# Attention groups with the shift added by TensorE and copied by ScalarE, and another order of the chunks at the end

## What is computed

```python
def _L1_xattn_ref(decoder_input, encoder_output, W_q, W_k, W_v, W_o, b_o):
    Q = (decoder_input @ W_q).reshape(B, Sd, HEADS, HEAD_DIM)      # 16 heads of 8
    K = (encoder_output @ W_k).reshape(B, Se, HEADS, HEAD_DIM)
    V = (encoder_output @ W_v).reshape(B, Se, HEADS, HEAD_DIM)
    scores = jnp.einsum('bqhd,bkhd->bhqk', Q, K) / jnp.sqrt(jnp.float32(HEAD_DIM))
    attn = jax.nn.softmax(scores, axis=-1)
    out = jnp.einsum('bhqk,bkhd->bqhd', attn, V).reshape(B, Sd, E)
    return out @ W_o + b_o

def _L1_ffn_ref(x, kernel, input_scale, kernel_scale, bias):
    x_q = (x / s_in).astype(jnp.float8_e4m3fn)
    k_q = (kernel / s_k).astype(jnp.float8_e4m3fn)
    y = jnp.dot(x_q, k_q) * (s_in * s_k)
    return y.astype(bfloat16) + bias
...
x = x + _L1_xattn_ref(_layernorm(x), ctx_1024, ...)
x = x + _L1_ffn_ref(_layernorm(x), ...)
```

## Time and profile before

| what | us |
|---|---|
| median of 3 runs | 194.49 |
| lowest and highest | 193.78 and 196.1 |
| the profiled execution | 194.31 |
| its span, first to last instruction | 192.5 |

### The profile page before, as it was taken

How to read it: one execution, slowest core, us unless ns; L and a number is a source line. 1 busy time by engine, 2 the same in 40 slices (tenths; PEclk the granted TensorE clock), 3 DMA queues, 4 the chain that set the end, 5 groups by cost and what they waited for, 6 DMA issues and landing times.

```text
span 192.5 us, 3676 instructions
## 1 busy us (share of the span) xinstructions
PE 173.8 (90%) x1301; PEld 131.7 (68%) x1301; DVE 138.2 (72%) x405; ACT 94.7 (49%) x170; POOL 48.1 (25%) x59
## 2 busy tenths in 40 slices
PE   4599999899999999999999999977999899889771
PEld 4289589678878888888788788553555565545540
DVE  2859757858556755585555697777999999977793
ACT  2357369554431332226322176567566657576252
POOL 3453356370400000028012136170221000002400
PEclk9969999999999999999999999999999999999978
DMA  5994000003084000000023000100230000000003
GB/s 192 370 420 178 2 3 2 0 0 112 3 200 124 5 0 0 0 3 0 0 67 89 11 0 2 58 0 0 73 95 5 0 0 5 0 3 0 0 0 109
DMA packets 5105, 10.26 MB, mean 53 GB/s; under 512 B 1472, under 2 KB 2752, under 8 KB 4800
## 3 DMA queue, kind: packets, MB, share of 16 engines
q1 hardware_dynamic: 3360, 9.44, 15.1%
q10 hardware_dynamic: 1728, 0.60, 1.2%
HBM read 6.37 MB, written 0.52 MB: 36 GB/s over the span
## 4 chain that ended last, share of the span: by engine, by line
PE 64%; issue 10%; DVE 10%; ACT 8%; DMA 4%; POOL 1%; SPq 1%; DVEq 0%; POOLq 0%; ACTq 0%
PE banks L1204 13%; PE bank L1020 6%; PE bank L1022 6%; PE bank L1021 6%; PE bank L1233 4%; DMA ctx<-in_ctx 4%; ACT raw L511 4%; ACT heads_out L519 2%; PE bank L1282 2%; PE banks L1020 2%; PE banks L1021 2%; PE banks L1022 2%; PE bank L1204 2%; PE bank L1273 2%; PE banks L1259 2%
## 5 line engine op out<-in xcount | busy, mean ns | idle before, releaser
L480 ACT ACTIVATE att<-bank 128x512 f32<-128x512 f32 x32 | 19.1, 598 | 46.0 <-PE bank L1022 33.1
L877 DVE TENSOR_REDUCE negm<-bank 128x2 f32<-128x512 f32 x61 | 39.1, 686 | 3.1 <-PE bank L1233 3.1
L511 ACT ACTIVATE raw<-banks 128x1024 f32<-128x1024 f32 x32 | 31.0, 1021 | 13.0 <-PE banks L1259 12.9
L277 POOL TENSOR_TENSOR rstd<-vpe,expo 128x4 f32<-128x4 f32 (+1 forms) x9 | 9.0, 998 | 56.0 <-DVE vpe L643 56.0
L1020 PE MATMUL bank<-xT,w 128*128 128x512 f32 x48 | 20.2, 420 | 0.7 <-DVE xT L774 0.7
L1233 PE MATMUL bank<-kst,w 32*128 32x256 f32 x122 | 20.1, 306 | 0.5 <-DVE negm L877 0.5
L1204 PEld LDWEIGHTS banks<-raw,attT 128*128 128x128 f32 x160 | 19.2, 192 | 1.2 <-issue 0.5
L1204 PE MATMUL banks<-raw,attT 128*128 128x128 f32 x160 | 19.7, 276 | 0.0
L1022 PE MATMUL bank<-xT,w 128*128 128x512 f32 x48 | 18.8, 392 | 0.0
L1021 PE MATMUL bank<-xT,w 128*128 128x512 f32 x48 | 18.8, 391 | 0.0
L845 DVE SCALAR_TENSOR_TENSOR xs<-banks,rw,xs 128x128 f32<-128x128 f32 x52 | 14.6, 344 | 5.7 <-PE banks L1204 5.6
(11 more groups left out here) (204 smaller groups left out, 328.5 us busy)
## 6 DMA issues: line engine op xcount, KB each, us to landing
raw<-in_w SPq DMA_DIRECT2D x1, 2048.0 KB, 10.8
raw<-kx SPq DMA_DIRECT2D x12, 128.0 KB, 2.6
raw<-qx SPq DMA_DIRECT2D x24, 64.0 KB, 2.1
raw<-in_w SPq DMA_DIRECT2D x1, 1024.0 KB, 8.5
xs<-in_x SPq DMA_DIRECT2D x2, 256.0 KB, 3.1
ctxT<-in_ctxT SPq DMA_DIRECT2D x1, 512.0 KB, 5.3
ctx<-in_ctx SPq DMA_DIRECT2D x1, 512.0 KB, 7.4
raw<-in_fixed SPq DMA_DIRECT2D x1, 512.0 KB, 4.0
```

The source lines that it names most:

```text
L480: act.activation(silus[:, k, :], bk[2 * k][:, :], ACT.Silu).then_inc(S["silu_s"], 1)
L511: act.activation(probs[:, m % 2, 2 * r:2 * r + 2, :, :].rearrange("p h k q -> p (h k q)"), pair[r][:, :], ACT.Exp, scale=ATT_SCALE).then_i ...
L877: dve.tensor_reduce(negm[:, m % 2, :, c0:c0 + 1].rearrange("p t c -> p (t c)"), bk[score_bank(m, r)][:, :].rearrange("p (t k) -> p t k", t ...
```

## The change

In a group, TensorE first lays the stacked queries into the bank of the turned maxima (a 256-column matmul with an fp32r identity, when the third maxima of the group are done), then adds the turned maxima to them as two ordinary matmuls. ScalarE copies the sum to `qa`, as the first thing of its group. The second and third scores stand directly behind the turned maxima, ahead of bank 7's work, and VectorE takes the second and third maxima together, ahead of the addition or the normalising. `o_copy(1)` stands ahead of the third normalisation in group 2. At the end the middle chunk goes ahead of the last one in every step, VectorE scales it (`middle_v`) in place of ScalarE, and the four `fill` matmuls between the chunks are gone.

```diff
-ORDER = (0, 2, 1)
+ORDER = (0, 1, 2)
...
+        identr = sb("identr", [P, P], r32)
...
+            act.copy(identr[:, :], ident).then_inc(S["identr_s"], 1)
...
+            def shifted(m):
+                act.wait_ge(S["mT_ps"], m + 1)
+                if m >= 2:
+                    act.wait_ge(S["s2_ps"], 2 * (m - 1))
+                act.copy(qa[:, m % 2, :], bk[turning(m)][:, 0:SEQ]).then_inc(S["qa_s"], 1)
+
             def act_group(m):
                 b, g = m // G, m % G
+                shifted(m)
                 if m == 1:
                     experts_out(UNITS - 2)
...
                 exps(m, 0)
                 exps(m, 1)
+                if m >= 2:
+                    o_copy(m - 1)
                 if m == 2:
                     for t in range(*HALVES[1]):
                         third_scaled(t)
-                if m >= 2:
-                    o_copy(m - 1)
...
             chunk_norm(1)
             turned_out(BATCH - 1)
-            chunk_v(1)
             chunk_overflow(0)
+            chunk_overflow(1)
             chunk_v(2)
             chunk_turned(0)
             chunk_overflow(2)
-            chunk_overflow(1)
             chunk_scaled(0)
+            chunk_turned(1)
             chunk_turned(2)
-            chunk_turned(1)
+            chunk_scaled(1)
             chunk_scaled(2)
-            chunk_scaled(1)
...
-            def shifted(m):
-                dve.wait_ge(S["mT_ps"], m + 1)
-                if m >= 2:
-                    dve.wait_ge(S["s2_ps"], 2 * (m - 1))
-                cols = slice(m // G * SEQ, (m // G + 1) * SEQ)
-                dve.tensor_tensor(qa[:, m % 2, :], bk[turning(m)][:, 0:SEQ], plain(qst[:, m % G, cols]), ALU.add)\
-                    .then_inc(S["qa_s"], 1)
...
                 if more:
                     maxima(m + 1, 0)
-                shifted(m)
                 if m == 2:
                     weigh_last()
                     sum_moments(HALVES[1])
                 if more:
-                    maxima(m + 1, 1)
+                    maxima(m + 1, 1, 2)
                 if g == 0 and b >= 2:
                     add_attention(b - 2, slice(TPB * (b - 2), TPB * (b - 1)))
                 if b > 0 and g in (1, 2):
                     normalise(b - 1, g - 1)
-                if more:
-                    maxima(m + 1, 2)
                 if m == G:
                     queries_lo(1)
                 if more:
...
+            def middle_v():
+                cols = slice(CHUNKS[1][0] * P, CHUNKS[1][1] * P)
+                dve.wait_ge(S["ln4_act"], TPB)
+                dve.tensor_scalar(fv[:, cols], f16[:, cols], rs[:, 0:1], None, ALU.mult).then_inc(S["fv1_s"], 1)
...
             chunk_power(0)
+            middle_v()
+            chunk_power(1)
             add_attention(BATCH - 1, slice(NT - TPB, NT))
             moments(4, CHUNKS[2], lambda t: dve.wait_ge(S["x3_s"], BATCH))
             chunk_rounded(0)
-            chunk_power(1)
+            chunk_rounded(1)
             scaled(4, 2, CHUNKS[2], f16t)
             chunk_overflowed(0)
             chunk_power(2)
             chunk_rounded(2)
-            chunk_rounded(1)
+            chunk_overflowed(1)
             chunk_overflowed(2)
-            chunk_overflowed(1)
...
+            def lay_queries(m):
+                pe.wait_ge(S["s1_max"], 4 * m + 3)
+                if m == 0:
+                    pe.wait_ge(S["identr_s"], 1)
+                    pe.wait_ge(S["hid_s"], HB * UNITS)
+                pe.matmul(bk[turning(m)][:, 0:SEQ], identr[:, :], qst[:, m % G, m // G * SEQ:(m // G + 1) * SEQ],
+                          start=True, stop=False)
+
             def turn_maxima(m):
                 pe.wait_ge(S["s1_max"], 4 * (m + 1))
-                if m == 0:
-                    pe.wait_ge(S["hid_s"], HB * UNITS)
                 for t in range(TPB):
-                    ins = pe.transpose(bk[turning(m)][:, t * P:(t + 1) * P], negm[:, m % 2, t, :], ident)
+                    ins = pe.matmul(bk[turning(m)][:, t * P:(t + 1) * P], negm[:, m % 2, t, :], ident,
+                                    start=False, stop=t == TPB - 1)
...
                 more, final = m + 1 < GROUPS, m == GROUPS - 1
+                lay_queries(m)
                 turn_maxima(m)
                 if more:
                     scores(m + 1, 1)
+                    scores(m + 1, 2)
                 bank7_used(m)
-                if more:
-                    scores(m + 1, 2)
...
             chunk_turn(0)
             chunk_product(0)
-            fill(6, 4)
+            chunk_turn(1)
             chunk_turn(2)
-            chunk_turn(1)
+            chunk_product(1)
             chunk_product(2)
-            chunk_product(1)
```

More of the change, by code:

```diff
@@ L203, in build @@
         names = """
-          ld_x0 ld_x1 ld_ctx ld_const ld_small ld_wc ld_fk ld_bl ld_wl ld_wg ld_w12 ld_w3 ld_att stored setup ident16_s v_zero w12_hi w12_lo k_ps k_out k_hi k_lo fixed staged0 staged1 staged2 staged3 kst_s qst_s
+          ld_x0 ld_x1 ld_ctx ld_const ld_small ld_wc ld_fk ld_bl ld_wl ld_wg ld_w12 ld_w3 ld_att stored setup ident16_s identr_s v_zero w12_hi w12_lo k_ps k_out k_hi k_lo fixed staged0 staged1 staged2 staged3 kst_s qst_s
           wg_hi wg_lo v_ps v_ev bl_added stats_s var_s mean_s rstd_s ln1     ln2
@@ L211, in build @@
           s1_ps s1_max mT_ps qa_s s2_ps p_s v_s pv_ps o_ev oT_ps den_s ao_s aoT_ps aoT_ev wo_ps x3_s
-          rs_s kv_s kovf_s fv_s q_s ovf_s f_s r_s r_pool nmr_s xq_s fT_ps fT_ev f_ps y_s
+          rs_s kv_s kovf_s fv_s fv1_s q_s ovf_s f_s r_s r_pool nmr_s xq_s fT_ps fT_ev f_ps y_s
           yz_s out_s""".split()
@@ L584, in chunk_v @@
                 cols = slice(CHUNKS[c][0] * P, CHUNKS[c][1] * P)
[L585 to L588, removed]
+                act.wait_ge(S["ln4"], TPH + TPB * (c // 2))
                 act.activation(fv[:, cols], f16[:, cols], ACT.Copy, scale=rs[:, 0:1]).then_inc(S["fv_s"], 1)
@@ L974, in shift @@
                     .then_inc(S["nmr_s"], 1)
+            def middle_v():
+                cols = slice(CHUNKS[1][0] * P, CHUNKS[1][1] * P)
+                dve.wait_ge(S["ln4_act"], TPB)
+                dve.tensor_scalar(fv[:, cols], f16[:, cols], rs[:, 0:1], None, ALU.mult).then_inc(S["fv1_s"], 1)
             def chunk_power(c):
                 cols = slice(CHUNKS[c][0] * P, CHUNKS[c][1] * P)
-                power_of_two(fv[:, cols], fe[:, cols], "fv_s", c + 1, 2 * (c + 1))
+                scaled_s, count = ("fv1_s", 1) if c == 1 else ("fv_s", c // 2 + 1)
+                power_of_two(fv[:, cols], fe[:, cols], scaled_s, count, 2 * (c + 1))
             def chunk_rounded(c):
```

## The result

The changed kernel takes 200.0 us (median of 4 runs, 199.66 to 200.94) against 194.1 us: ratio 1.032, 95% interval 1.028 to 1.037. It is slower, where 193.8 us had been forecast. The profiled execution (200.94 us, the longest of the four) has a span of 199.2 us.

The account below looks back on a forecast made before the run. Two near-equal loops, ScalarE's through the third scores and VectorE and TensorE's through the turn, were taken to bound the attention groups. Attention +0.85 and the end -1.4 gave -0.55 us: 193.8 us, range 191.0 to 196.2.

Parts of the forecast that it names:

- two loops of nearly one length: Attention groups: ScalarE's loop through third scores to exponentials; the turn, scores, maxima, `ao`, outputs loop with 0.18 us slack.
- The order: Groups 5 to 15: normalising after third maxima starts outputs 0.24 to 0.3 us later; period 3.82 us against 3.64.
- The kind with g = 3: A batch's group where nothing is normalised: the turn comes 1.14 us behind the outputs' start, period 3.04 us.
- The turned maxima are ordinary matmuls now ... So I count nothing.: TensorE's turn: ordinary fp32 matmuls take 0.12 us against 0.11 for transposes, so no cost; at most 0.05 for weight loads.
- With 0.12 us for that matmul.: Queries' matmul on TensorE, ahead of the turn: 0.12 us taken, between bounds of 0.11 and 0.31.
- Rival 2: TensorE between outputs and second scores pays the added matmul in full: 0.29 us more a group, 197.2 us; chance 0.13.
- Rival 3: At the turn, maxima as ordinary matmuls cost four times a transpose: +7.9 us, 201.7 us; chance 0.02.
- Rival 1: ScalarE's loop stays the limit in the attention groups: 0.14 us a group gained, 191.3 us; chance 0.28.
- The end, -1.4 us: Last chunks: without the fill holding TensorE, VectorE's last addition ends at 188.82 instead of 190.23.
- -0.4 from the order remains: The end: if the removed fill matmuls weren't the holder, the new chunk order alone still saves 0.4 us.
- 0.9 fills it and delays nothing: The end: middle chunk's scaling and power of two, 0.9 us, fit VectorE's 0.97 us wait before L904.
- Groups 0 to 4: Early groups, TensorE the limit: sum's copy delays group 2's last unit by 0.71; about -0.2 us by group 5's turn.

Follow-up runs that it names:

- order_only: Kernel before, with only second and third scores together on TensorE and second and third maxima together on VectorE: ratio 1.001.
- lay_only: Kernel before, with only the queries' matmul added ahead of each turn, its result overwritten by the transposes: ratio 0.999.
- turn_matmul: Kernel before, with only the turned maxima made by ordinary matmuls in place of transposes: ratio 1.006.
- order_turn_matmul: Kernel before, with the new order of second and third scores and maxima plus turned maxima as ordinary matmuls: ratio 1.013.
- early_third: Kernel before, with only TensorE's third scores moved ahead of bank 7's work, VectorE's order kept: 192.4 us, ratio 0.987.
- order_lay: Kernel before, with the new order of second and third scores and maxima plus the queries' matmul, overwritten by the transposes: ratio 1.010.
- end_only: Kernel before, with only the changed end (middle chunk first, its scaling on VectorE, no fill between the chunks): ratio 1.0015.
- after_pool_later: Changed kernel, with GpSimd's addition for chunk 0 waiting until the middle chunk's power of two is made: 199.0 us, ratio 1.029.

## Why the prediction was wrong

*What bounds the kernel before.* Right: two loops of nearly one length. The 1.02 us from the outputs to the next full-array matmul and the 0.18 us of slack are borne out by order_only and lay_only.

*The order.* Right in mechanism, and in size for the groups that it walked through: 3.82 us a group had been worked out with 0.12 for the queries' matmul, so 3.70 without it; order_only has 3.76. `ao` ended 2.68 behind the turn there, where the text had 2.63. The kind with g = 3 was too cheap: 3.04 - 0.12 = 2.92 had been said, and order_only has 3.16. In all the text has 36.34 - 1.2 = 35.1 us for groups 5 to 15 with the order alone, and 36.1 were measured.

*"The turned maxima are ordinary matmuls now ... So I count nothing."* This is the step that failed. The 0.12 us that I took for an ordinary fp32 matmul came from "1.98 us for 16", and I took the 16 rows for 16 matmuls. Line 1204 issues 8, not the 16 that the text on the kernel has: four tiles, two halves of the hidden features. Each is two rows in the trace, so 0.23 us against 0.11 for a transpose. Everything needed stood in view: x16 in the row, two loops in the code. The trace of before even has the very case, the two ordinary fp32 matmuls of `output_layer`, with the 0.71 us that the turn takes in turn_matmul:

```profile
146.81 0.71 PE L1295 MATMUL bank<-wo,aoT 128*128 128x128 f32 x4 [0.19 <-ACT heads_out L519]
```

The same holds for the outputs, 8 calls and 16 rows; there it did no harm, because the duration was taken as a whole. Worth 0.22 to 0.27 us in each group, 2.7 us in groups 5 to 15 (order_turn_matmul).

*"With 0.12 us for that matmul."* Measured 0.22 up to the turn. The upper bound of 0.31 had been dropped with the reason that it is already in the 1.02; that was half right. With both measured terms the period of 3.82 becomes 3.82 + 0.10 + 0.22 = 4.14; measured 4.15. So in groups with g = 1 or 2 the two are the whole error. From group 5 to 15 the forecast was 36.3 us and 40.0 were measured: 2.7 of the 3.7 us are these two terms (order_only to the changed kernel took 3.9 where 1.2 had been counted), 1.0 is the order, above.

*Rival 2* (TensorE pays in full, 197.2 us) came nearest: the right place, its sign (0.23 us from the queries' matmul to the turn, over 0.2) seen, and 0.29 us a group where 0.33 was measured. But it had 0.19 more for the queries and 0.1 for the turn where 0.10 and 0.22 were measured, so the near sum is partly luck, and its 197.2 us is still 2.8 short and outside the range given. I had given it 0.13, on the ground of rows 8, the misread ones. *Rival 3* (four times a transpose, 201.7 us) had the other half of the truth: the turned maxima are dearer, but twice, not four times. The Trainium skill ("TensorE: Matmul & The Clock Gate", section Terms) gives the transposing mode as four times as fast for FP32; I set this aside because the rows "contradict it". They did not: rows 2 and 8, rightly counted, give a factor of two. The measurement decides against the four, but the rule's direction was right, and I had counted nothing.

*Rival 1* (the ScalarE loop, 191.3 us): false for the whole change. Its 0.14 us a group is there to be had only if normalising isn't put off, and then in part: early_third.

*The end, -1.4 us.* Measured -0.4 between the two profiles, and +0.3 against an unchanged end with the clock in full. Two terms failed. The fill looked expensive (2.06 us for four) because that execution had TensorE's clock at half there; a window's granted clock would have told. With the clock in full it held nothing up (lay_only). The text's own way out, "-0.4 from the order remains", is what is left with the collision gone: 16.2 against 16.65 us. Its sum doesn't come out either: the terms listed from 186.07 on, with five handovers of 0.05, end at 188.6, not at 188.82. And "0.9 fills it and delays nothing" forgot who else was at work: GpSimd's addition (178.9 to 180.2 in the profile of before) runs in the very 0.97 us that VectorE has free. The Trainium skill says in "SBUF — State Buffer", section "SBUF: two separate sides", that VectorE in a two-port mode and GpSimd share a pair of ports under an exclusive lock, held for a whole instruction. The traces agree: 1.26 us for 0.29, ending 0.15 us behind GpSimd's, and 0.29 again once GpSimd starts later. What they don't show by themselves is that the port is the reason.

*Groups 0 to 4.* The copy ahead of the last unit's was foreseen and is seen; taking it back gave 0.5 us. But from the turn of group 0 to that of group 5 there are 23.3 us against 22.6, so +0.7 where -0.2 had been forecast. The same two terms are behind most of it: over this stretch turn_matmul alone has +0.7 and lay_only +0.4, where the text had counted 0.24 for both; order_only has -0.5.

*The sum.* Groups 5 to 15 account for 3.7 us of the error, groups 0 to 4 for 0.9, group 15 for 0.2 (-0.3 instead of -0.5), the end for 1.0: 5.8 of the 6.2 us between 193.8 and 200.0.

*The other things that the text asked to see*: the outputs start behind `ao` at 2.90 us from the turn (156.59 - 153.69), 2.7 had been said, the difference being the longer turn. No wait for maxima beyond the 0.41 us of above stands ahead of the turn. The last chunk's transposes start 0.06 us behind their L745, within the 0.1 that was said. Groups 5 to 15 took 40.0 us, not less than 34.8, but also not 36.3.

## What to carry to other kernels

Before a matmul is priced from a row, count the calls in the source against the rows in the trace: an fp32 128x128 matmul that isn't a transpose had two rows and cost twice as much here. Reordering can be nearly free alone (1.001) and still take away the slack that had hidden other edits; then price every added piece on the engine that becomes the limit in full (1.0 and 0.0 us became 2.7 and 1.7). Look at what the other engines do in an idle stretch before work is moved into it, and at the granted clock before a slow row is called expensive.

## What the runs showed of the hardware

- An ordinary fp32 128x128 matmul: two rows 0.11 us apart, loads of 192 ns (turn_matmul). A transpose: one row, loads of 140 ns (before).
- A 256-column fp32r matmul on 128 rows with weights of its own: 0.22 to 0.23 us to the next matmul's start behind the outputs (32-column tiling), 0.20 to 0.26 behind `down`, 0.11 to 0.13 behind the 512-column `fill` (lay_only, order_lay, the changed kernel and its variants). What makes the difference wasn't tested.
- A VectorE `tensor_scalar` of 128x256 in 32 bits, started 0.28 us behind a GpSimd addition of 128x512, took 1.26 us instead of 0.29, in the changed kernel and in end_only. A VectorE addition of 128x256 with one operand in PSUM, overlapped by a GpSimd addition, took its 0.42 us, in after_pool_later (185.73 to 186.15, GpSimd from 185.84) and in the kernel before (179.71, GpSimd 178.89 to 180.17).
